# Thirty blocks instead of thirty-six store plain rows, and the step scheduler's durations are read from a trace

## The reference

```
h   = layernorm(x)
agg[dst] += (h @ W)[src] * rsqrt(out_deg[src])        # 106250 edges, sorted by dst
x   = x + relu(agg * rsqrt(in_deg) + b)
z   = layernorm(x);  probs = softmax(z @ Wr + br);  two best experts, weights renormalised
y_e = gelu((layernorm(z) * ln_g[e] + ln_b[e]) @ W1[e] + b1[e]) @ W2[e] + b2[e]   # 256 -> 1024 -> 256
out = x + w1 * y_{e1}[node] + w2 * y_{e2}[node]
```

## Time and profile before

| | us |
|---|---|
| median of 3 runs | 1815.56 |
| lowest and highest | 1807.80, 1820.68 |
| the profiled execution's own time | 1821.93 |
| its span, first to last instruction | 1820.4 |
| mean granted TensorE clock | 0.808 |

### The profile page before, as it was taken

The page is one execution under the profiler, slowest core; times in us unless marked ns, Lnnn a source line. Parts: engine busy times, 40 slices in busy tenths (PEclk is TensorE's granted clock), DMA queues, the critical chain, the costliest instruction groups (busy, mean ns, idle before and its releaser), DMA issues.

```text
span 1820.4 us, 26707 instructions
## 1 busy us (share of the span) xinstructions
PE 1227.2 (67%) x9012; PEld 994.4 (55%) x9012; DVE 979.5 (54%) x2657; ACT 613.3 (34%) x1218; POOL 1102.3 (61%) x1112
## 2 busy tenths in 40 slices
PE   0692657686428645886498558959948965777990
PEld 0692436454217323774387447838736754666980
DVE  0899456655615453557256636656564743654440
ACT  0865211111005102433144214514414642444660
POOL 2100777777777777777777777777773105662334
PEclk9999755556559756997699769969978987889995
DMA  4005877765356436774577467766756557887761
GB/s 144 26 2 142 283 248 237 244 194 171 103 192 195 117 106 214 254 248 133 190 257 264 137 199 262 251 224 225 235 163 196 206 179 257 289 256 207 250 193 18
DMA packets 147233, 350.99 MB, mean 193 GB/s; under 512 B 25768, under 2 KB 95946, under 8 KB 130712
## 3 DMA queue, kind: packets, MB, share of 16 engines
q1 hardware_dynamic: 86204, 205.79, 33.1%
q0 software_dynamic: 54528, 137.10, 25.7%
q10 hardware_dynamic: 6364, 6.40, 1.1%
HBM read 291.21 MB, written 59.89 MB: 193 GB/s over the span
## 4 chain that ended last, share of the span: by engine, by line
DMA 30%; PE 28%; POOL 18%; issue 11%; DVE 8%; ACT 3%; SPq 1%; DVEq 0%; POOLq 0%; ACTq 0%
DMA gt<-zt,srcI 17%; POOL gt L719 11%; PE ps L1029 7%; PE ps L1108 6%; DMA out<-gt,toks 6%; PE ps L1123 5%; DMA S<-ys,cidx 4%; PE ps L998 4%; POOL xs L735 4%; PE ps L1041 2%; DMA idx<-in_dst 2%; POOL S L751 2%; POOL out L765 2%; PE ps L1062 1%; PE ps L1071 1%
## 5 line engine op out<-in xcount | busy, mean ns | idle before, releaser
L719 POOL DMA_INDIRECT gt<-zt,srcI x832 | 832.9, 1001 | 257.5 <-issue 174.6
L1029 PE MATMUL ps<-gt,S 128*128 128x257 f16 x1664 | 366.9, 338 | 339.1 <-DMA gt<-zt,srcI 337.5
L1029 PEld LDWEIGHTS ps<-gt,S 128*128 128x128 f16 x1664 | 203.3, 153 | 459.3 <-DMA gt<-zt,srcI 441.7
L1108 PE MATMUL ps<-xe,w1b 128*128 128x256 f16 x2688 | 341.9, 281 | 41.6 <-DVE xe L1517 41.5
L982 ACT ACTIVATE h<-ps,cb 128x256 f32<-128x256 f32 x448 | 227.5, 558 | 361.9 <-PE ps L1108 354.6
L1123 PE MATMUL ps<-w2b,hT 128*128 128x256 f16 x2688 | 325.6, 280 | 18.6 <-DVE gt L1540 17.7
L1108 PEld LDWEIGHTS ps<-xe,w1b 128*128 128x128 f16 x2688 | 270.3, 101 | 82.2 <-DVE xe L1517 45.2
L1123 PEld LDWEIGHTS ps<-w2b,hT 128*128 128x128 f16 x2688 | 269.8, 101 | 57.5 <-issue 18.4
L1523 DVE SCALAR_TENSOR_TENSOR hT<-h,cb,hT 128x512 f16<-128x512 f32 x224 | 166.9, 748 | 175.9 <-ACT hT L986 175.1
L1235 DVE TENSOR_TENSOR S<-dlo,irun 128x1024 f16<-128x1024 f16 x104 | 71.1, 684 | 183.5 <-PE ps L1029 183.0
L735 POOL DMA_INDIRECT xs<-xrow,slI x98 | 99.8, 1019 | 111.7 <-DVE slI L1311 83.0
(11 more groups left out here) (261 smaller groups left out, 1213.0 us busy)
## 6 DMA issues: line engine op xcount, KB each, us to landing
w1b<-ws SPq DMA_DIRECT2D x56, 1024.0 KB
w2b<-ws SPq DMA_DIRECT2D x56, 1024.0 KB, 7.5
ws<-w2b SPq DMA_DIRECT2D x16, 1024.0 KB, 4.9
xb<-xs SPq DMA_DIRECT2D x56, 258.0 KB, 4.7
gt<-zt,srcI POOLq DMA_INDIRECT x832, 3.2
ys<-yb SPq DMA_DIRECT2D x36, 256.0 KB, 6.1
w1b<-in_L_ffn_W SPq DMA_DIRECT2D x8, 1024.0 KB, 8.9
hT<-in_L_ffn_W SPq DMA_DIRECT2D x8, 1024.0 KB, 13.7
```

What stands on the lines that cost most here:

```text
L719: e.indirect_dma_start(out=gt[:, i % NG, :], out_offset=None, in_=zt, in_offset=bass.IndirectOffsetOnAxis(ap=srcI[:, c, r:r + 1].bitcast(u ...
L1029: inst = e.matmul(PS[r % 2][:, 0:257], S[:, r % NS, :, c], gt[:, i % NG, part * 257:part * 257 + 257], start=(c == 0 and part == 0), stop= ...
L1108: inst = e.matmul(UP[n % 2][:, z * BS:(z + 1) * BS], w[:, l, kk, j * 128:(j + 1) * 128], xe[m % 2][:, k, kk, :], start=(kk == 0 and l == 0 ...
```

## The change

A constant `EARLY = LAST - 3` takes the place of `LAST - 2`. So M0 is 30 and not 36, TG is 37 and not 43, and NA is 26 and not 20. `r9` runs for chunks 0 to 4 and no longer for chunk 5. All buffers, rings and instructions stay as they are. Besides, the assumed costs in `plan()` are other numbers.

```diff
-M0 = FULL[LAST - 2]
-TG = CHUNKS[LAST - 2][1]
+EARLY = LAST - 3
+M0 = FULL[EARLY]
+TG = CHUNKS[EARLY][1]
 NA = NB - M0
 NQ = 8
...
-        chain = [("wa", ex, (("PE", 1.0), ("DVE", 2.6))), ...
+        chain = [("wa", ex, (("DVE", 2.8), ("PE", 4.0))), ...
...
-    yield [[("nd1", g, (("DVE", 1.4),))]]
-    yield [[("nT", t, (("PE", 0.8), ("ACT", 0.4))), ("nW", t, (("PE", 1.1),)), ("hh", t, (("DVE", 1.6),))] for t in range(a0, a1)]
+    yield [[("nd1", g, (("DVE", 2.6),))]]
+    yield [[("nT", t, (("PE", 0.3), ("ACT", 0.4))), ("nW", t, (("PE", 0.9),)), ("hh", t, (("DVE", 1.7),))] for t in range(a0, a1)]
...
-    yield [[("xT", t, (("PE", 0.8), ("ACT", 0.4))), ("lg", t, (("PE", 0.3),)), ("lr", t, (("DVE", 0.25),))] for t in range(a0, a1)]
+    yield [[("xT", t, (("PE", 0.3), ("ACT", 0.4))), ("lg", t, (("PE", 0.3),)), ("lr", t, (("DVE", 0.25),))] for t in range(a0, a1)]
...
-           + ([("r9", c, (("DVE", 1.2 + 0.1 * CHUNKS[c][1]),))] if c <= LAST - 2 else [])]
+           + ([("r9", c, (("DVE", 2.0 + 0.13 * CHUNKS[c][1]),))] if c <= EARLY else [])]
...
-            end = emit("turn", m, (("PE", 1.4), ("ACT", 0.7)), s["now"])
+            end = emit("turn", m, (("PE", 0.55), ("ACT", 0.65)), s["now"])
-            end = emit("up", (m, q), (("PE", 1.4), ("ACT", 1.9)), s["now"])
+            end = emit("up", (m, q), (("PE", 1.35), ("ACT", 1.85)), s["now"])
-            end = emit("down", (m, h), (("PE", 2.8),), s["now"])
+            end = emit("down", (m, h), (("PE", 2.65),), s["now"])
...
-            emit("tile", i, (("PE", 0.3),), s["now"])
+            emit("tile", i, (("PE", 0.25),), s["now"])
-        emit("add", r, (("DVE", 1.0),), s["now"])
+        emit("add", r, (("DVE", 1.2),), s["now"])
...
-                    if c == LAST - 2:
+                    if c == EARLY:
                         then(e.tensor_scalar(pidx[:, :, :], pidx[:, :, :], float(M0 * BS), None, ALU.add))
```

More of the change, by code:

```diff
@@ L105, in weight_stages @@
     for ex in range(E):
-        chain = [("wa", ex, (("PE", 1.0), ("DVE", 2.6))), ("wb", ex, (("DVE", 2.8),)), ("wc", ex, (("PE", 0.2),)),
+        chain = [("wa", ex, (("DVE", 2.8), ("PE", 4.0))), ("wb", ex, (("DVE", 2.8),)), ("wc", ex, (("PE", 0.2),)),
                  ("wd", ex, (("DVE", 0.5),)), ("we", ex, (("PE", 0.2),)), ("wf", ex, (("DVE", 2.8),)),
```

## The result

The changed kernel takes 1854.56 us (median of 4 runs, 1850.63 to 1854.76) against 1816.67 us of the kernel before on the same chip: ratio 1.0215, 95% interval 1.0184 to 1.0247. It is 2.1% slower; 1778 us were forecast, with a range up to 1818. The profiled execution has a span of 1852.8 us, 32.4 us over the span before. All lines are one higher than before (719 is 720, 735 is 736, 1540 is 1541).

The account below looks back on a forecast made before the run. POOL's issuing was taken to bound the edge loop, then the first `give`'s start to decide. Span 1820.4 - 94.0 (earlier first `give`) + 56.8 (six more steps) = 1783.2 us, adjusted +1.5 - 6.4 to 1778 us; range 1750 to 1818.

Parts of the forecast that it names:

- The new costs in `plan()`: Edge loop: they move steps, but POOL's ring of 16 gathers gives 21 us of slack; taken at 0, bounds -6 and +15 us.
- The start of the fetch back: POOL behind the edge loop: waits for block 29, so the first gather starts at 1404.1 us, 109.0 us earlier.
- Its length: Fetch back on POOL: 37 tiles take 108.3 us, plus 15.6 us for 12 scatters and 17 us for node work on DVE.
- Draining: Between the fetch back and the first `give` on POOL: stays at 14.1 us.
- `give` steps: End of the kernel on POOL: six more at 9.47 us each beside running blocks, +56.8 us, bounds 36 and 63 us.
- The stream of blocks: PE's blocks during the fetch back: keep nearly level with the `give` chain, block 38 at some 1570 us against 1568.
- rival C: Blocks starve as combines waiting for gathers hold up `low` or `split`: block 38 at 1622 us, time 1835 us; chance 0.12.
- C's own sign: During the fetch back, PE idles before line 1108 by more than some 30 us.
- D: Fetch-back gathers lengthen beside added DVE work, each to the longest measured: 35 us more, time 1813 us; chance 0.04.
- the stretch that the prediction quoted beside it: Fetch-back gathers: VectorE's two-port mode locks GpSimd out, 620 ns alone, 3100 beside a copy; over 100 us more, not expected.
- The split's worth by itself: Tail: first `give` 94.0 us earlier, less 56.8 us for six more `give` steps.

Follow-up runs that it names:

- e1: Changed kernel with all assumed costs in `plan()` as in the kernel before, so the split alone; ratio 0.9946 to the kernel before.
- e4: Changed kernel, each chunk's first scatter listed no sooner than 14 us of model time behind `r5` while edge tiles are left; ratio 0.9791 to the kernel before.
- e9: Kernel before with its chunk scatters held back by 14 us of the list's time behind `r5` while edge tiles are left; ratio 0.9733 to the kernel before.
- e2: New assumed costs alone, with 36 plain blocks and 43 tiles fetched back as in the kernel before; ratio 1.0196 to the kernel before.
- f2: Split at 30 plain blocks with old assumed costs except new ones for node and router work; ratio 1.0043 to the kernel before.
- e6: Changed kernel with the last chunk's eight blank stores sent without waiting for one another; ratio 1.0026 to the kernel before, against 1.0112 for the changed kernel.
- b0: Kernel before, unchanged, run for its trace on a slower chip; ratio 1.00 by its making.
- g1: Split at 30 plain blocks, old assumed costs, scatters held back 15 us and blank stores sent together; ratio 0.9681 to the kernel before.
- g2: Kernel before (36 plain blocks, old costs) with scatters held back 14 us and blank stores sent together; ratio 0.9683 to the kernel before.
- e5: Changed kernel with SP's stores of combined tiles issued six combines later; ratio 1.0118 to the kernel before, against 1.0112 for the changed kernel.
- e1b: Changed kernel with all assumed costs old, run again beside the changed kernel; ratio 0.9928 to the kernel before.

## Why the prediction was wrong

Span forecast 1783.2, measured 1852.8 us; the 69.6 us by the steps of the sum:

- **The new costs in `plan()`, taken at 0 (bounds -6 and +15): +40.8 us, the step that failed.** The bounds came from what POOL waits for in front of gathers and from its ring of 16. The ring protects POOL against a late PE. It doesn't protect it against its own list: POOL executes in order, and a scatter ahead of its routing stops every gather behind it. The two waits for `slI` in front of scatters, 3.62 and 0.89 us in the trace before, were not among the rows read; they showed that the list had hardly any margin there. What the trace shows in place of the 0 is 38.9 us more of standing. The place moved by 7 and 8 edge tiles at chunks 2 and 3 (471 to 464, 592 to 584; some 9 and 10 us at 1.3 us a gather). At chunks 4 and 5 it moved by only 2, but their routing was done 31.4 and 40.1 us later than before, while POOL came to them 21.0 and 30.7 us later. Why the routing came so late is not shown.
  The standing on the first chip is read from its trace. That the costs bring it and not the split follows from the orders, since e1's order up to the last gather is that of the kernel before. e4 and e9 show on other chips that taking the standing away brings the last gather forward by 55.8 us for 64.5, and 51.8 for 67.3. On those chips the costs lose 2.0% by another way (e2), with the standing unchanged; waits of POOL for PE are longer there (f2), which on the first chip they aren't.
- **The start of the fetch back: right.** 17.9 us behind the last gather against 19.3. Block 29's `y` starts 10.7 us behind it, as before.
- **Its length, 140.9 with 15.6 us of scatters and 17 us of node work: right, 136.6.** Coupling through the combines was there (waits of 9.02 and 7.50 us), of the size taken. DVE was busy 69% of the stretch, where over 75% were forecast. The half taken between two bounds was a choice, and luck has a part in its fit: the slower chips gave 143 to 172 us for the stretch.
- **Draining, left at 14.1: +21.8 us.** Blank stores were charged to the loads and not to the `out` stores that stand in the same queue. Before, they had finished before any combine store was due; the earlier fetch back put the two together. e6 takes 17.5 of 21.3 us of surplus away (35.4 to 17.9, with 14.1 in b0). The old costs with the same split have 24.6 (e1), so the rest of the surplus hangs on where the list puts the blanks.
- **`give` steps, +56.8: +11.7 us over that.** The count was right: 19 intervals instead of 13 lie ahead of the last `y`. They take 9.92 us each and not 9.47, which makes 8.6 us, with the DMA engines 0.75 busy and not 0.69; the last step to the end took 11.8 us instead of 8.7. On other chips the same six steps more cost 60.8 us (e1 against b0) and 60.2 us (g1 against g2), so the rate was nearly right.
- **The stream of blocks: rival C's number, and half its mechanism.** Block 38's `y` starts at 1627.46 us, C said 1622. C had DVE's combines, which wait for their gathers, hold up PE through `low` and `split`. They did hold it up, for 31.3 us, but through the routing of chunk 7: PE stands for `Mb`, and DVE has combines with waits of 3.97, 2.59 and 4.83 us in front of it. The other 25.7 us are a block load behind the blanks on SP's queue. C's own sign, PE idle by more than 30 us in that stretch, was there. e5 shows that the combine stores aren't to blame.
- Gathers did not lengthen: their mean is 977 ns against 1013. So neither D appeared nor the stretch that the prediction quoted beside it.

The split's worth by itself, forecast at 37 us, was 0.5 to 0.7%, some 11 to 15 us, where the list still stood (e1, e1b), and in the repaired lists none that shows (g1 against g2: medians 1.1 us apart). Most of the gain at one end is taken back at the other: each `give` moved into the tail costs 10 us beside running blocks.

## What to carry to other kernels

Assumed costs that are read from a trace don't by themselves make a better order: here they lost 2%. Each engine's margin in front of its in-order waits has to be read again. Before a cost is changed, list every wait of the bounding engine by what it waits for, also the small ones in front of rare instructions; those with the least slack decide. When a stage moves earlier, look on every queue that it uses for what it will now meet. And when a repair doesn't show where it was expected, look at the other stretches before calling it off the path: the blanks cost at the first `give` in one kernel and at the first fetch in the other.

## What was not expected of the hardware

Four chips ran the kernel before in 2049 to 2067 us and the first in 1817, 13 to 14% apart. The same order of instructions stands 4.5 us ahead of its scatters on the first and 70.5 us on the fourth. On the slower ones a gather takes no longer on POOL (987 against 1001 ns), but 410.0 us instead of 257.5 lie before the 832 of them, and 90.9 us of that end by a release that the trace names only as remote. What slows them there was not found. Eight small stores that wait for each other took 18.22 to 32.98 us over all these traces, and 8.28 to 11.91 us when sent together.
